# Two sums of an expert layer's partial results as strided reductions on VectorE, and a swap of two of its steps

## The reference

```python
w = jax.nn.softmax(masked, axis=-1)                 # tokens x 16 experts
def moe_proj(p):
    y = jnp.einsum('nc,ech->neh', x, p)
    return jnp.einsum('ne,neh->nh', w, y)
q, k, v = moe_proj(q_proj), moe_proj(k_proj), moe_proj(v_proj)
attn = softmax(q @ k.T / sqrt(h))                   # within a sequence
o = attn @ v
z = jnp.einsum('ne,nh->enh', w, o)
out = jnp.einsum('enh,ehc->nc', z, o_proj)          # the sum that the change is about
x = x + jnp.tanh(g_ffn[1]) * out
```

## Time and profile before

| | |
|---|---|
| median of three runs | 1622.75 us (1621.93 to 1623.85) |
| profiled execution, its own time | 1619.88 us |
| its span in the trace | 1618.2 us |
| granted TensorE clock, mean | 0.977 of full |
| PE busy | 1499.3 us (93% of the span) |
| DVE busy | 1285.3 us (79%) |
| POOL busy | 1186.7 us (73%) |
| ACT busy | 1103.2 us (68%) |

### The profile page before, as it was taken

How to read it: one execution, slowest core, us unless ns; L and a number is a source line. 1 busy time by engine, 2 the same in 40 slices (tenths; PEclk the granted TensorE clock), 3 DMA queues, 4 the chain that set the end, 5 groups by cost and what they waited for, 6 DMA issues and landing times.

```text
span 1618.2 us, 52841 instructions
## 1 busy us (share of the span) xinstructions
PE 1499.3 (93%) x17129; PEld 1304.2 (81%) x17130; DVE 1285.3 (79%) x4046; ACT 1103.2 (68%) x2757; POOL 1186.7 (73%) x1715
## 2 busy tenths in 40 slices
PE   6888888866999789999999999999999999999996
PEld 4666666646999479888888888888888889889985
DVE  4777777754555378988999989988998999988885
ACT  4888888843556457677676776677667766776664
POOL 4666666632455568888888888888888888888785
PEclk9999999977999899999999999999999999999998
DMA  3221222225543000000000000000000000000000
GB/s 81 86 65 65 65 65 65 79 83 130 146 137 85 27 15 15 21 15 15 21 20 16 15 21 16 20 15 21 15 22 15 17 19 21 15 15 18 5 7 11
DMA packets 85963, 64.84 MB, mean 40 GB/s; under 512 B 11888, under 2 KB 81552, under 8 KB 85776
## 3 DMA queue, kind: packets, MB, share of 16 engines
q1 hardware_dynamic: 70368, 45.13, 9.6%
q0 software_dynamic: 5120, 12.62, 2.5%
q10 hardware_dynamic: 10288, 4.74, 1.1%
HBM read 35.74 MB, written 22.52 MB: 36 GB/s over the span
## 4 chain that ended last, share of the span: by engine, by line
PE 80%; issue 7%; DVE 6%; POOL 2%; ACT 2%; DMA 1%; SPq 0%; POOLq 0%; DVEq 0%; ACTq 0%
PE s_bank L2016 12%; PE s_bank L2018 11%; PE s_bank L2017 11%; PE tb L1833 7%; PE s_bank L1951 4%; PE po L1963 4%; PE s_bank L1813 4%; PE po L1847 3%; PE m L1784 2%; PE s_bank L2164 2%; PE s_bank L1822 1%; PE m L1863 1%; DVE qkv L1567 1%; PE m L1767 1%; PE s_bank L2151 1%
## 5 line engine op out<-in xcount | busy, mean ns | idle before, releaser
L746 POOL TENSOR_TENSOR qkv<-qkv,scaled 128x384 f32<-128x384 f32 x480 | 489.3, 1019 | 85.3 <-ACT scaled L1032 36.1
L1032 ACT ACTIVATE scaled<-s_bank,wg 128x384 f32<-128x384 f32 x449 | 260.2, 584 | 114.7 <-PE s_bank L2018 110.1
L2016 PE MATMUL s_bank<-proj_hi,hn_hi 128*128 128x384 f32 x900 | 327.3, 364 | 5.4 <-DVE qkv L1567 5.4
L1567 DVE SCALAR_TENSOR_TENSOR qkv<-s_bank,wg,qkv 128x384 f32<-128x384 f32 x449 | 273.7, 610 | 51.0 <-PE s_bank L2018 41.0
L2018 PE MATMUL s_bank<-proj_hi,hn_lo 128*128 128x384 f32 x900 | 302.5, 336 | 0.0
L2017 PE MATMUL s_bank<-proj_lo,hn_hi 128*128 128x384 f32 x900 | 301.6, 335 | 0.0
L900 ACT ACTIVATE pT<-tb 128x512 f32<-128x512 f32 x256 | 154.6, 604 | 111.2 <-PE tb L1833 110.5
L1833 PE MATMUL tb<-ident,prob 128*128 128x128 f32 x1024 | 162.9, 283 | 46.3 <-issue 30.5
L2016 PEld LDWEIGHTS s_bank<-proj_hi,hn_hi 128*128 128x128 f32 x900 | 169.5, 188 | 18.8 <-DVE qkv L1567 14.0
L1833 PEld LDWEIGHTS tb<-ident,prob 128*128 128x128 f32 x1024 | 119.6, 145 | 71.3 <-issue 63.1
L2017 PEld LDWEIGHTS s_bank<-proj_lo,hn_hi 128*128 128x128 f32 x900 | 170.0, 189 | 1.6
(11 more groups left out here) (288 smaller groups left out, 3753.5 us busy)
## 6 DMA issues: line engine op xcount, KB each, us to landing
xs<-sorted_in SPq DMA_DIRECT2D x71, 128.5 KB, 2.1
sorted_out<-yo SPq DMA_DIRECT2D x71, 64.0 KB, 1.6
xin<-in_x SPq DMA_DIRECT2D x32, 128.0 KB, 2.1
cin<-in_ctx SPq DMA_DIRECT2D x32, 128.0 KB, 2.4
ctx_cols<-xcT SPq DMA_DIRECT2D x32, 128.0 KB, 1.8
w<-in_L_ffn_W SPq DMA_DIRECT2D x16, 256.0 KB
xcT<-ctx_cols SPq DMA_DIRECT2D x32, 128.0 KB, 2.8
kx<-kT SPq DMA_DIRECT2D x128, 32.0 KB
```

The source lines that it names most:

```text
L746: g.tensor_tensor(into, into, scaled[m % SCALED][:, 0:cols], ALU.add).then_inc(dense_added, 1)
L1032: ins = act.activation(into, bank[:, 0:3 * D], ACT.Copy, scale=wg[v % 4][:, 1, k:k + 1])
L1567: v.scalar_tensor_tensor(out=acc, in0=bank[:, 0:3 * D], scalar=wg[w % 4][:, 0, k:k + 1], in1=acc, op0=ALU.mult, op1=ALU.add).then_inc(dens ...
L2016: pe.matmul(bank[:, 0:cols], hi[:, tile], of(proj_hi), start=True, stop=False)
```

## The change

`total_groups` becomes one `tensor_reduce` that reads all four groups of `sums` (512 elements a partition, the group innermost, so that consecutive reads lie 512 bytes apart) and writes the 128 sums of tile 1 straight into `oall[:, 1, :]`. `total` becomes one `tensor_reduce` over the two halves of tile 0 (256 elements, read in the same way) that writes `oall[:, 0, :]`. `halves` loses the part that held tile 1. Since `total_groups(u - 2)` now overwrites `oall`, it waits for `result(u - 3)`, and the two calls change places.

```diff
-        halves = sb("halves", [P, 2, 2, D])
+        halves = sb("halves", [P, 2, D])
...
-                            into, cols = halves[:, 0, e % 2, :], slice(D * (e % 4), D * (e % 4) + D)
+                            into, cols = halves[:, e % 2, :], slice(D * (e % 4), D * (e % 4) + D)
...
             def total_groups(w):
                 if exists(w):
                     v.wait_ge(dense_added, added_no(w + 1, "o", 3) + 1)
-                    v.tensor_tensor(halves[:, 1, :, :], sums[:, 0:2, :], sums[:, 2:4, :], ALU.add)\
+                    wait(v, f["res_ready"], w)
+                    v.tensor_reduce(oall[:, 1, :], sums[:, :, :].rearrange("p g n -> p n g"), AX_X, ALU.add)\
                         .then_inc(f["sum_steps"], 1)
 
             def total(w):
                 if exists(w):
                     v.wait_ge(f["row_sums"], E1 * w + E1)
-                    v.wait_ge(f["sum_steps"], 2 * w + 1)
                     wait(v, f["res_ready"], w)
-                    v.tensor_tensor(oall[:, :, :], halves[:, :, 0, :], halves[:, :, 1, :], ALU.add)\
+                    v.tensor_reduce(oall[:, 0, :], halves[:, :, :].rearrange("p g n -> p n g"), AX_X, ALU.add)\
                         .then_inc(f["sum_steps"], 1)
...
                 take(u, "q", 3, 4)
+                result(u - 3)
                 total_groups(u - 2)
-                result(u - 3)
                 token_weights(u - 1)
```

## The result

The changed kernel takes 1627.62 us (median of 6 runs, 1625.59 to 1629.56), the kernel before 1622.57 in the same comparison (6 runs). The ratio is 1.0026, with a 95% interval of 1.0015 to 1.0037: slower by 5 us, where the forecast was 2. The profiled execution took 1627.22 us, with a span of 1625.5 for 1618.2 before; the mean granted clock is 0.977 in both.

What follows compares the result with a forecast made beforehand. PE was taken as the bound, DVE counting only where PE waits for it. Steady passes -1.5, last passes +3.2, second place 0 and end +0.3 gave +2.0 us on 1622.75: 1624.7 us, range 1620 to 1631.

Steps and rivals of the forecast that it cites:

- the passes at the edge: Passes 28 to 31: the later product on pbd meets POOL's additions, +3.2 us in all.
- the second place: Sum of the two halves of tile 0: reduction of 0.61 us for an addition of 0.71, worth 0.

Runs made afterwards that it cites:

- experiment 6: Part 5 taken ahead of the token weights, in the kernel with reductions in passes 2 to 27 and the old additions from 28; 1625.97 us, ratio 1.0024.
- experiment 5: Part 5 taken ahead of the token weights, in the kernel before the change; 1638.85 us, ratio 1.0109.
- experiment 3: The changed kernel with the group sum ahead of the result again, and two buffers for oall; 1654.41 us, ratio 1.0189.
- experiment 10: As experiment 6, with parts 6 and 7 also taken ahead of the gate's lower limit; 1611.57 us, ratio 0.9924.
- experiment 7: The changed kernel with 20 more reductions of sums in ten forms behind its last result; one run, 1641.03 us.
- experiment 4: As experiment 2, with one more four-group reduction into a spare tile ahead of the group sum in passes 2 to 27; 1651.62 us, ratio 1.0170.
- experiment 2: The changed kernel with the additions and order of before from pass 28 on; 1619.60 us, ratio 0.9975.
- experiment 12: The kernel before, with the reductions and changed order only from pass 28 on; 1625.25 us, ratio 1.0022.

## What to carry over

Before an operation on a nearly idle-free engine is made longer or shorter, look for what holds the steps behind it. A step held by another engine ends when that engine lets go, and its own start can move for free within that room, here 1.36 us in most steady passes and 0.3 in the last ones (0.31 by the earlier trace rows). Look at the passes at the edge apart: they held the whole loss. And when a wait stems from a step that can be held, put the work that the bottleneck waits for ahead of it, and of every other such step behind it as well: moving one part cost 0.2% and 1.1% against the kernel before (experiments 6 and 5), moving two or three gained 0.5 to 0.75%.

## What the runs showed of the hardware

- A VectorE step with two SBUF operands that is issued 0.35 us into a gather of POOL is not served at the gather's end when POOL's next addition follows 0.03 us later. It waits for the addition too: 2.00 us for a step of 0.48 (experiment 3). The Trainium skill ("SBUF — State Buffer", section "SBUF: two separate sides") calls the port that the two share an exclusive lock, held by whichever starts first for its whole instruction. The rows agree on the whole instruction for additions (1.09 us for the product behind a 1.01 us addition). On who comes first they add that the step that had already waited 0.67 us did not get its turn in between. Between two additions, 0.15 us apart, a held step does: the product ends 0.29 behind the first. For the gather they show an exception to the whole instruction. In pass 20 of the kernel before, the product is issued 0.08 us behind the gather's start and isn't held:

```profile
1228.47 1.02 POOL L601 DMA_INDIRECT xin<-sorted_out,placei  x1 [0.96 <-issue]
1228.55 0.42 DVE L1546 TENSOR_TENSOR pbd<-pbd,srs 128x256 f32<-128x256 f32 x1
```

- Reductions, with their one operand, were never held: 0.42 us at the second place in 27 passes beside POOL's additions. A tensor_scalar of 128x2 elements was: 0.99 us, issued 0.26 us behind the start of an addition, against 0.18 issued 0.15 us before the end of a POOL step (experiments 6 and 10).
- A reduction pays 0.32 to 0.37 us for 512 fp32 elements when it walks four or more separate inputs, 0.04 for 384 elements with three, nothing for 256 with two (experiment 7).
- The same idle time of PE in pass 30, 2.02 to 2.04 us, was followed by matmuls of about 0.52 us for some 3 us, at a granted clock of 0.50, in the executions of six kernels (the changed one, experiments 3 to 7), and by matmuls of 0.34 at a granted clock of 1.00 in those of three others (experiments 2, 10 and 12).
